# The alignment stage of a two-layer Perceiver kernel: norms taken from reciprocals, squares on one engine, a reload on another queue, and five flag instructions rewritten

## The reference, cut to what matters

```
def _pairwise_euclidean(a, b):           # a = ctx of one batch (257 rows), b = normed x (32 rows)
    aa = jnp.sum(a * a, axis=-1)[:, None]
    bb = jnp.sum(b * b, axis=-1)[None, :]
    return jnp.sqrt(jnp.maximum(aa + bb - 2.0 * (a @ b.T), 0.0))
def _align_one(small, large):            # _L1_xattn_ref(ctx_1024, _layernorm(x))
    D = _pairwise_euclidean(small, large)
    R = _dtw_cost(D)                     # R[i,j] = D[i,j] + min(R[i-1,j], R[i,j-1], R[i-1,j-1])
    i_idx, j_idx, valid = _backtrack(R, T_small, T_large)   # argmin of (diagonal, up, left)
    contrib = small[i_idx] * valid[:, None]
    return jnp.zeros((T_large, d)).at[j_idx].add(contrib)
```

## Time and profile before

| | |
|---|---|
| median of 3 runs | 1983.76 us (1981.63 to 1995.86) |
| profiled execution | 1991.11 us, its span 1989.3 us |
| busy over the span | PE 1734.4 (87%), PEld 840.6 (42%), DVE 1122.2 (56%), ACT 660.5 (33%), POOL 770.0 (39%) |
| mean granted clock | 0.904 |
| chain that ended last, by engine | PE 51%, POOL 20%, DVE 13%, issue 11%, ACT 2%, DMA 2% |

### The profile page before, as it was taken

The page is one execution under the profiler, slowest core; times in us unless marked ns, Lnnn a source line. Parts: engine busy times, 40 slices in busy tenths (PEclk is TensorE's granted clock), DMA queues, the critical chain, the costliest instruction groups (busy, mean ns, idle before and its releaser), DMA issues.

```text
span 1989.3 us, 22637 instructions
## 1 busy us (share of the span) xinstructions
PE 1734.4 (87%) x8392; PEld 840.6 (42%) x8392; DVE 1122.2 (56%) x1523; ACT 660.5 (33%) x1176; POOL 770.0 (39%) x427
## 2 busy tenths in 40 slices
PE   7888886996999999999998858999821889899998
PEld 4666653551332332332333525444410556654443
DVE  2444443178998999998996233222349464521211
ACT  1333331152554554554553131111312240111121
POOL 1333330205998998998997010000200006000000
PEclk8999997896999999999998768999865879889999
DMA  2111101011000000000000500111063100101110
GB/s 71 33 32 32 32 22 51 0 50 52 12 14 20 10 15 21 11 15 21 10 9 15 219 0 0 32 47 32 0 132 82 32 0 1 43 1 42 43 42 21
DMA packets 34944, 65.51 MB, mean 33 GB/s; under 512 B 12740, under 2 KB 21848, under 8 KB 33188
## 3 DMA queue, kind: packets, MB, share of 16 engines
q1 hardware_dynamic: 34868, 64.49, 11.0%
HBM read 55.80 MB, written 8.67 MB: 32 GB/s over the span
## 4 chain that ended last, share of the span: by engine, by line
PE 51%; POOL 20%; DVE 13%; issue 11%; ACT 2%; DMA 2%; SPq 0%; DVEq 0%; ACTq 0%; POOLq 0%
POOL arena L1006 19%; PE ps L1226 6%; PE ps L1998 6%; PE ps L1987 6%; PE ps L198 4%; PE ps L1239 3%; PE ps L339 3%; PE ps L344 3%; PE ps L221 2%; DVE arena L934 2%; PE ps L357 2%; DVE arena L474 2%; PE ps L1762 2%; PE ps L1778 1%; PE ps L787 1%
## 5 line engine op out<-in xcount | busy, mean ns | idle before, releaser
L1006 POOL TENSOR_TENSOR arena<-arena 128x1024 f32<-128x1024 f32 x248 | 577.8, 2399 | 26.6 <-DVE arena L960 18.2
L787 PE MATMUL ps<-arena 32*128 32x512 f32 x2016 | 473.3, 643 | 24.8 <-DVE arena L941 19.3
L892 ACT ACTIVATE arena<-arena 128x1024 f32<-128x1024 f32 x248 | 262.2, 1057 | 296.7 <-DVE arena L950 296.7
L963 DVE TENSOR_TENSOR arena<-arena,ps 128x1024 f32<-128x1024 f32 x248 | 302.3, 1219 | 9.9 <-POOL arena L1006 8.8
L950 DVE TENSOR_TENSOR arena<-arena,ps 128x1024 f32<-128x1024 f32 x248 | 301.0, 1214 | 10.2 <-PE ps L787 10.2
L787 PEld LDWEIGHTS ps<-arena 32*128 32x128 f32 x2016 | 164.0, 189 | 335.5 <-issue 143.1
L811 PE MATMUL ps<-arena 128*32 128x512 f32 x1024 | 140.4, 621 | 5.2 <-DVE arena L963 3.1
L1226 PE MATMUL ps<-arena 128*128 128x512 f32 x288 | 131.9, 603 | 0.6 <-ACT arena L1291 0.6
L2079 DVE TENSOR_TENSOR arena<-arena,ps 128x512 f32<-128x512 f32 x56 | 38.5, 688 | 160.7 <-ACT arena L2041 160.7
L1944 POOL TENSOR_TENSOR arena<-arena 128x1024 f32<-128x1024 f32 x16 | 29.9, 1895 | 226.6 <-DVE arena L1877 213.3
L1987 PE MATMUL ps<-arena 128*128 128x512 f32 x256 | 116.6, 600 | 0.0
(11 more groups left out here) (275 smaller groups left out, 2221.2 us busy)
## 6 DMA issues: line engine op xcount, KB each, us to landing
arena<-ctxT SPq DMA_DIRECT2D x32, 257.0 KB, 3.1
arena<-ctxT SPq DMA_DIRECT2D x8, 1028.0 KB, 15.4
arena<-L_ffn_w SPq DMA_DIRECT2D x16, 512.0 KB, 4.2
arena<-ctx_rows SPq DMA_DIRECT2D x8, 960.0 KB
m_rows<-arena SPq DMA_DIRECT2D x16, 256.0 KB, 2.6
arena<-m_rows SPq DMA_DIRECT2D x64, 64.0 KB
arena<-L_ffn_eW SPq DMA_DIRECT2D x8, 512.0 KB, 3.6
m_yd<-arena SPq DMA_DIRECT2D x64, 32.0 KB
```

The costliest lines, as they stand in the source:

```text
L787: mm = nc.tensor.matmul(ps[:, ring(n) + jj, :], weights[r], m_row[r, buf, t % CH, :], start=True, stop=True)
L892: nc.scalar.activation(m_xa[:, u, t % 2], m_xa[:, u, t % 2], ACT.Exp, scale=-1.0).then_inc(S["m_dec"], 1)
L963: nc.vector.tensor_tensor(m_h[:, u, t % 2], m_xa[:, u, t % 2], ps[:, ring(n):ring(n) + 2, :], ALU.add).then_inc(S["m_use"], 1)
L1006: nc.gpsimd.tensor_tensor(m_xa[:, u, t % 2], m_xa[:, u, t % 2], m_h[:, u, (t - 1) % 2], ALU.mult).then_inc(S["m_kept"], 1)
```

## The change

Four edits, all in the alignment stage. (a) bb is worked out from n_r by two DVE instructions on 128 x 8 values; the squaring of the normed x on ACT, the 16 pairs on PE and the copy from PSUM go. (b) All eight squares are made on ACT; d_pool does nothing. PE waits for a tile's squares between its two groups of 16 matmuls rather than ahead of both. ACT's order becomes squares 0, centred 0 and 1, deviation 0, squares 1, deviation 1, squares 2 to 7, then the roots. (c) SyncE only writes the tiles out; `back` is issued on ACT's queue, back(g - 2) behind root(g), with four semaphores in turn instead of two. SyncE waits for all of d_back before the loads of ctx_rows. (d) The flags: DVE makes stay (no move up), then dg = dg * stay and lf = stay - dg, and ACT makes up = 1 - stay.

```
-        ACT_SQ = 5
+        d_stay = bview(11296, SLOTS, WW)
...
         def d_load(sp):
-            def keep(g):
+            for g in range(TT):
                 sp.wait_ge(*S.at("d_sqrt", 2 * g + 2))
-                sp.dma_start(dist[:, g * P:(g + 1) * P].rearrange("k p i -> p k i"), d_dt[g]).then_inc(S[f"d_out{g % 2}"], 16)
...
-            keep(0)
-            for g in range(1, TT):
-                keep(g)
-                back(g - 1)
-            back(TT - 1)
-            sp.wait_ge(*S.at("d_ab", TT))
+                sp.dma_start(dist[:, g * P:(g + 1) * P].rearrange("k p i -> p k i"), d_dt[g]).then_inc(S[f"d_out{g % 4}"], 16)
+            sp.wait_ge(*S.at("d_back", 16 * SEG * TT))
...
             def tile(g):
-                if g < ACT_SQ:
-                    pe.wait_ge(*S.at("d_sq", g + 1))
-                else:
-                    pe.wait_ge(*S.at("d_ss", g - ACT_SQ + 1))
...
+                pe.wait_ge(*S.at("d_sq", g + 1))
                 for k in range(DC):
...
-            tile(0)
-            pe.wait_ge(*S.at("d_tsq", 1))
             for g in range(TT):
-                for k in range(DC):
-                    mm = nc.tensor.matmul(ps[:, 4, g:g + 1], U[2][:, k, g * P:(g + 1) * P], ones[:, 0:1],
-                                          start=(k == 0), stop=(k == 1))
-            mm.then_inc(S["d_bb"], 1)
-            for g in range(1, TT):
                 tile(g)
...
+            deviation(0)
             squares(1)
-            for h in range(NH):
-                deviation(h)
-            squares(2)
-            act.wait_ge(*S.at("dn_out", 2))
-            nc.scalar.activation(U[2], U[1], ACT.Square).then_inc(S["d_tsq"], 1)
-            squares(3)
-            root(0)
-            squares(4)
-            for g in range(1, TT):
+            deviation(1)
+            for g in range(2, TT):
+                squares(g)
+
+            def back(g):
+                act.wait_ge(*S.at(f"d_out{g % 4}", 16 * (g // 4) + 16))
+                for k in range(SEG):
+                    r = slice(B * k + SL * g, B * k + SL * g + SL)
+                    act.dma_start(d_D[r, k:k + L].rearrange("p j i -> p (j i)"),
+                                  dist[k, g * P:(g + 1) * P].rearrange("(b j) i -> b (j i)", j=L)).then_inc(S["d_back"], 16)
+            for g in range(TT):
                 root(g)
+                if g >= 2:
+                    back(g - 2)
+            back(TT - 2)
+            back(TT - 1)
...
+            act.wait_ge(*S.at("d_sort", 1))
+            nc.scalar.activation(by_slot(2)[:, :, 1:WW], d_stay[0:PB, :, 1:WW], ACT.Copy, bias=1.0,
+                                 scale=-1.0).then_inc(S["d_up"], 1)
...
-            dve.wait_ge(*S.at("d_bb", 1))
-            ch.link(nc.vector.tensor_copy(d_bb, ps[:, 4, 0:TT]))
+            ch.link(nc.vector.tensor_tensor(d_bb, n_r, n_r, ALU.mult))
+            ch.link(nc.vector.tensor_scalar(d_bb, d_bb, -D * 1e-5, float(D), ALU.mult, ALU.add))
...
-            ch.link(nc.vector.scalar_tensor_tensor(out=up[:, :, own], in0=dg[:, :, own], scalar=-TINY,
-                                                   in1=least[:, :, W:0:-1], op0=ALU.mult, op1=ALU.is_ge))
-            ch.step(nc.vector.scalar_tensor_tensor(out=lf[:, :, own], in0=dg[:, :, own], scalar=0.0,
-                                                   in1=up[:, :, own], op0=ALU.is_equal, op1=ALU.is_gt))
-            ch.sync()
-            ch.link(nc.vector.tensor_tensor(dg[:, :, own], dg[:, :, own], up[:, :, own], ALU.is_gt))
+            nc.vector.scalar_tensor_tensor(out=stay[:, :, own], in0=dg[:, :, own], scalar=-TINY,
+                                           in1=least[:, :, W:0:-1], op0=ALU.mult, op1=ALU.is_lt).then_inc(S["d_sort"], 1)
+            dve.wait_ge(*S.at("d_sort", 1))
+            ch.link(nc.vector.tensor_tensor(dg[:, :, own], dg[:, :, own], stay[:, :, own], ALU.mult))
+            ch.link(nc.vector.tensor_tensor(lf[:, :, own], stay[:, :, own], dg[:, :, own], ALU.subtract))
+            dve.wait_ge(*S.at("d_up", 1))
...
         def d_pool(pool):
+            return
```

More of the change, by code:

```diff
@@ L65 @@
          + [(3, "tile_qblk", "d_ms", TT), (3, "tile_norm", "d_tm", TT), (3, "tile_rec", "d_add", TT)]
-         + [(3, "once_3", "d_m2", 1), (3, "once_4", "d_bb", 1), (3, "once_5", "d_tsq", 1)]
+         + [(3, "once_3", "d_m2", 1), (3, "once_4", "d_up", 1)]
          + [(4, "once_1", "t_ss", 1), (4, "once_2", "t_root", 1), (4, "once_3", "t_oT", NH), (4, "once_4", "t_ln", NH)]
@@ L1642, in d_dve @@
                 dve.wait_ge(*S.at("d_fwd", 3 * s + 3))
-            own = slice(1, WW)
+            own, stay = slice(1, WW), d_stay[0:PB]
             ch.step(nc.vector.tensor_tensor(dg[:, :, W:0:-1], R[:, 0:SLOTS, 0:W], R[:, 0:SLOTS, own], ALU.is_le))
             ch.link(nc.vector.tensor_tensor(least[:, :, own], R[:, 1:SLOTS + 1, 0:W], least[:, :, own], ALU.subtract))
-            ch.link(nc.vector.scalar_tensor_tensor(out=up[:, :, own], in0=dg[:, :, own], scalar=-TINY,
-                                                   in1=least[:, :, W:0:-1], op0=ALU.mult, op1=ALU.is_ge))
-            ch.step(nc.vector.scalar_tensor_tensor(out=lf[:, :, own], in0=dg[:, :, own], scalar=0.0,
-                                                   in1=up[:, :, own], op0=ALU.is_equal, op1=ALU.is_gt))
-            ch.sync()
-            ch.link(nc.vector.tensor_tensor(dg[:, :, own], dg[:, :, own], up[:, :, own], ALU.is_gt))
+            nc.vector.scalar_tensor_tensor(out=stay[:, :, own], in0=dg[:, :, own], scalar=-TINY,
[4 more added lines that the diff above has]
+            dve.wait_ge(*S.at("d_up", 1))
             for k in range(SEG - 1):
```

## The result

The changed kernel takes 1979.93 us in the median of 20 runs (1973.82 to 1989.53), the kernel before 1990.8 in 20 (1981.63 to 2008.54). The ratio is 0.9947, 95% interval 0.993 to 0.9965: 10.6 us faster (7.0 to 13.9), where 9.4 were forecast. The 1974.3 of the forecast hung on a median of three runs, 1983.76; with 20 runs the kernel before stands 7 us higher, and the changed kernel's 1979.93 is 5.6 above the forecast.

The account below looks back on a forecast made before the run. Not PE but a serial chain, ending in 29 us of SyncE's write-outs and reloads, was taken as the bound. -7.9 and -1.5 sum to -9.4, from 1983.76 to 1974.3 us; range 1968 to 1985.

Parts of the forecast that it names:

- the sum: Alignment stage: -7.9 us up to DVE's first recurrence step and -1.5 in the flags, together -9.4.
- no fall of the clock: PE's distance tiles: without single columns the clock rises at about 1437.6 and stays; 1.73 us a tile, 3.65 at low clock.
- the table load ran ahead of the variance: ACT's deviation 0: its 1.28 us table load starts once ACT is free, at 1424.95, not when the variance is there.
- the 0.6 of the sum: Norm: products end at 1431.6 rather than 1432.25, so PE starts 0.6 us earlier; +0.3 if the table load waited.
- 3 us for the clock: Later stages: untouched, but PE's clock changes fall at other places, some 3 us either way.
- 2.7 us a tile between 2.4 and 3.15: Reloads: pace taken as 2.7 us a tile, giving -7.9; with 2.4 it is -10.3, with 3.15 -4.3.
- 1.8 for start and landing: Reload stream: start-up and landing some 0.9 us each, added to eight tiles' transfers.
- ACT's 1.4 us a tile: ACT's queue: 0.5 us for a tile's two roots and 0.92 for three issues, less than the transfers' 2.4.
- the engines stay fed: Reloads on ACT: ACT's 1.4 us a tile is below the transfers' 2.4 at least, so transfer engines never lack work.
- 2.65 in the prediction: Reloads: busy us a tile on each of the four loaded transfer engines, some 85% busy at the old pace.
- The rule that speaks against (c): Reloads: a second issuer saves issue time only, so the pace stays 3.15 us a tile and the sum is -5.8.
- Dear issues on ACT: Rival, 0.05: ACT's 24 reload issues cost more than SyncE's 0.31 each; even at 1.1 us, 1993.0 at 1.5.

Follow-up runs that it names:

- one pair of profiles: Changed kernel with the squares of tiles 5 to 7 back on GpSimd, profiled beside the changed kernel: first reload 23.9 against 25.3, first step 49.0 against 50.3.
- the four-tile kernel: Changed kernel, but tiles read back four at a time, 16 rows to a transfer: first step 44.4, ratio 0.9949; run again, 44.0, 1975.08 us, ratio 0.9925.
- the edited kernels with ACT's order: Follow-up kernels with reloads issued on ACT, among them the changed kernel with columns, old flags or GpSimd squares back: first steps 56.4, 51.4, 49.0.
- the small transfers: Against the kernel reading four tiles at a time: same two issue points, but 24 reloads of 4 rows, not 6 of 16; first step 55.6, ratio 0.9977.
- columns back: Changed kernel with the 16 pairs of single-column matmuls put back after tile 0, their result unused: first step 56.4, ratio 0.999.

## Why the prediction was right, point by point

**Size.** Forecast -9.4, measured -10.6 (7.0 to 13.9). In the three profiles of the changed kernel the stage is 6.9 to 9.2 shorter than in the one of before: 5.2 to 7.5 at the first step, where the sum had 7.9, and 1.5 in the flags. The gain of half a per cent is there. The 1.4 to 3.7 us between the stages and the medians are not accounted for, and that -9.4 lies so near to -10.6 is partly luck.

**Part (a) was the larger part**, 5.2 alone. The mechanism was as worked out: one stall less for the tiles, and no fall of the clock. The last group starts 15.3 after the first matmul now, 20.3 before.

**Part (b), the norm:** the table load ran ahead of the variance, as I took it:

```profile
1420.51 1.06 ACT L1514 ACTIVATE arena<-arena 128x1024 f32<-128x1024 f32 x1 [0.66 <-DVE arena L250]
1421.59 1.28 ACT L1519 ACT_TABLE_LOAD   x1
1422.88 0.26 ACT L1519 ACTIVATE arena<-ps,arena 128x4 f32<-128x4 f32 x1
```

(the second profile of the changed kernel). PE's first matmul moved from 16.4 to 15.3 where the clock was alike, 1.1 against the 0.6 of the sum. But in two of the three profiles it stood at 18.6, since both of the norm's first groups met more of the low clock: the means took 6.67 and the variances 5.73 us in the chain above, 5.21 and 3.94 in the second profile (granted clock 0.55 and 0.62 over the two groups, against 0.70 and 0.93). Three of the 14 profiles of the study have the slow norm, all three with ACT's new order; the means' matmuls, slow already, start ahead of anything that the change moved, so whether it has a part in this is open. I had allowed 3 us for the clock, but only in later stages; in this stage it stood at nothing. That is the term that was mis-sized. The sum puts the first reload at 26.5 and the first step at 49.9 from the stage's start. In the two profiles with the slow norm the first step came 2.3 and 2.7 later than that, and 1.8 and 1.6 of it were there at the first reload; with the fast norm the reload came 1.2 earlier and the step 0.4 later. The roots' place behind the squares was in the sum, as the date of write-out 0, but without a price of its own; it is some 1.3 by one pair of profiles.

**Part (c), the pace:** I took 2.7 us a tile between 2.4 and 3.15. By the same sum, with its 1.8 for start and landing, which no run measures by itself, the changed kernel has 2.76, 2.90 and 2.84. ACT's 1.4 us a tile counted its issues and roots but not its waits, and these held roots 6 and 7. But "the engines stay fed" came out all the same. The profile gives the packets of each DMA queue, their number, MB, and their time as a share of 16 engines; q10 appears only where ACT issues the reloads and has their 1.07 MB, and q1 has SyncE's write-outs. First from 1437 to 1465, then while ACT waited for write-out 3 (1445.14 to 1450.45):

```profile
q1 hardware_dynamic: 3200, 1.07, 15.7%
q10 hardware_dynamic: 192, 1.07, 15.5%
```
```profile
q1 hardware_dynamic: 793, 0.27, 21.7%
q10 hardware_dynamic: 46, 0.25, 17.9%
```

15.5% of 16 engines over 28 us are 69 engine-us, 8.7 a tile, or 2.2 on each of four; the write-outs add 8.8 a tile, 0.55 on each of 16. Together the four have 2.7 us of work a tile, against 2.65 in the prediction and a pace of 2.76. During ACT's wait the reloads' share was 17.9%, near the 18.2% of the whole stretch from first reload to first step (18.1 and 16.6 against 18.2 and 18.1 in the other two profiles). If four engines carry them, these four were 93% busy in the wait, write-outs included, and 87% over the stretch. So the waits made roots late, but no row shows that they starved the transfers. What would have won more was to spread the same bytes, as the four-tile kernel did.

**The rule that speaks against (c)** was the Trainium skill's, "DMA: Bandwidth & Descriptors", section "Issuing engines are not separate DMA queues". It holds in that both issuers feed the same engines: SyncE's write-outs took up to 8.5 us to land with ACT's reloads of four rows in flight, and at most 5.6 with its reloads of 16 rows. What it would make of the time, no change of pace, the runs contradict: part (c) is worth 3 to 4 us. What SyncE's stream did before shows where time was to be won. Root 7 and write-out 7:

```profile
1455.97 0.33 ACT L1547 ACTIVATE arena<-arena 128x172 f32<-128x172 f32 x1
1463.63 0.38 SPq L1433 DMA_DIRECT2D dist<-arena  x1
```

The write-out stood 7.3 us behind waits for earlier write-outs, where after the change SyncE issued it at once. That this wait is the whole of the 3 to 4 us is argued, not shown: part (c) also holds back the loads of ctx_rows and has four semaphores for two, and no run parts them. The last reload landed in 5.7 to 6.0 us with those loads behind it, in 4.5 to 5.2 in the three profiles of the changed kernel, so up to 1.5 us can be theirs; in the edited kernels with ACT's order it took 4.7 to 6.4, so that too is open.

The rule of the same page of the Trainium skill by which a transfer of four rows goes to four engines ("Why a DMA increments its semaphore by 16 and not by 1") was the useful one: the small transfers' first step at 55.6 against 44.4 agrees with it, with 2.8 of the 11.2 us due to the number of issues.

**Part (d):** -1.50 forecast, 14.55 to 13.05 measured, with ACT's 2.7 at 2.64. **Dear issues on ACT:** 0.25 to 0.32 us each in the chain, so that rival was off.

## What to carry to other kernels

Ask how many transfer engines a reload uses before asking which queue issues it: a busy share near 0.2 while transfers are queued hints that a few engines carry all, and more rows to a transfer was worth more here (6 to 8 us) than a second queue (3 to 4). A wait placed on a computing engine's stream holds what stands behind it, but before you move the wait, look whether the transfers ran dry meanwhile: here they had not, and placing small reloads behind the roots gained nothing (55.6 against 50.3 to 52.6). And price a few slim matmuls between wide ones with the clock of what follows them.

## What was not expected of the hardware

The same single columns (16 pairs in the program, 32 matmuls in the trace) took 3.89 us in one profile and 6.99 in another, by the granted clock they met. In one program the clock rose at their start (before), in another it stayed low through them and 4 us beyond (columns back), with the same tile of matmuls ahead of them. And two profiles of one and the same kernel differed by 3.2 us within the first 19 us of the stage, 1.5 in the matmuls of the means and 1.8 in those of the variances, by the granted clock they met.
